# Expert blocks of a routed feed-forward layer as two 64-row halves, each with an expert of its own

## The reference

```
logits = einsum('th,eh->te', x, gate_w)            # 1024 tokens, 16 experts
scores = softmax(logits); topk_w, topk_idx = top_k(scores, 2)
combine = sum(one_hot(topk_idx, E) * topk_w[..., None], axis=1)
gu = einsum('th,ehj->etj', x, w_gate_up)           # 256 -> 2 x 176
h  = silu(gu[..., :I]) * gu[..., I:]
y  = einsum('eti,eih,te->th', h, w_down, combine)  # 176 -> 256
y  = y + swiglu(x @ shared_gate_up) @ shared_down
```

## Time and profile before

| | us |
|---|---|
| median of 3 runs | 252.67 (252.64 to 252.76) |
| profiled execution | 252.71 |
| its span, first to last instruction | 250.7 |
| PE / PEld busy | 237.4 / 177.2 |
| DVE / ACT / POOL busy | 148.5 / 129.3 / 92.5 |

### The profile page before, as it was taken

How to read it: one execution, slowest core, us unless ns; L and a number is a source line. 1 busy time by engine, 2 the same in 40 slices (tenths; PEclk the granted TensorE clock), 3 DMA queues, 4 the chain that set the end, 5 groups by cost and what they waited for, 6 DMA issues and landing times.

```text
span 250.7 us, 5232 instructions
## 1 busy us (share of the span) xinstructions
PE 237.4 (95%) x1660; PEld 177.2 (71%) x1660; DVE 148.5 (59%) x452; ACT 129.3 (52%) x465; POOL 92.5 (37%) x110
## 2 busy tenths in 40 slices
PE   8969799999999999999999999799999999999995
PEld 6635475666766677898788787567777777777784
DVE  1568888887889856437896588653223232323184
ACT  2146988989889898540524216124343434343440
POOL 2111211112111100102662004655777777777460
PEclk9999999999999999999999999999999999999999
DMA  7999877100005400006013000222333333343495
GB/s 217 267 366 387 283 174 171 53 3 3 3 0 160 171 3 3 1 3 229 1 41 129 0 3 4 63 68 81 105 105 107 105 95 112 89 102 111 144 338 188
DMA packets 20388, 28.10 MB, mean 112 GB/s; under 512 B 2369, under 2 KB 17355, under 8 KB 20363
## 3 DMA queue, kind: packets, MB, share of 16 engines
q1 hardware_dynamic: 16683, 19.01, 24.5%
q0 software_dynamic: 2976, 8.13, 11.0%
q10 hardware_dynamic: 704, 0.64, 0.8%
HBM read 21.61 MB, written 6.16 MB: 111 GB/s over the span
## 4 chain that ended last, share of the span: by engine, by line
PE 71%; ACT 13%; DVE 8%; issue 4%; DMA 1%; POOL 1%; ACTq 0%; POOLq 0%; DVEq 0%
PE bank L898 15%; PE bank L910 11%; ACT pr_s L1010 10%; PE bank L829 8%; PE bank L531 5%; PE bank L573 4%; PE bank L560 3%; PE bank L879 3%; PE bank L889 3%; PE bank L658 2%; PE bank L536 2%; PE bank L623 2%; PE bank L649 1%; PE bank L668 1%; DMA qx_s<-ffn_in,prT 1%
## 5 line engine op out<-in xcount | busy, mean ns | idle before, releaser
L1010 ACT ACTIVATE pr_s<-bank,mx 128x128 f32<-128x128 f32 x128 | 45.2, 383 | 8.0 <-DVE mx L1236 8.0
L898 PE MATMUL bank<-gu_s,bxT 128*128 x124 | 41.7, 460 | 0.2 <-DVE bxT L1561 0.2
L1567 DVE TENSOR_TENSOR pr_s<-bank,pr_s 128x176 f32<-128x176 f32 x31 | 10.6, 341 | 51.6 <-ACT pr_s L1165 50.9
L492 POOL DMA_INDIRECT expert_out<-by,prT x31 | 31.0, 1000 | 14.8 <-ACT by L1000 7.5
L487 POOL DMA_INDIRECT qx_s<-ffn_in,prT x31 | 30.1, 972 | 14.6 <-issue 8.2
L1000 ACT ACTIVATE prT<-bank 128x512 f32<-128x512 f32 (+1 forms) x63 | 31.1, 497 | 2.9 <-PE bank L573 1.8
L910 PE MATMUL bank<-dn_s,prT 88*128 x124 | 31.7, 379 | 0.0
L1010 ACT ACTIVATION_READ_ACCUMULATOR pr_s<-bank,mx 128x1 f32 x128 | 28.6, 224 | 0.0
L898 PEld LDWEIGHTS bank<-gu_s,bxT 128*128 128x128 f32 x124 | 21.2, 190 | 7.2 <-issue 0.4
L1000 ACT ACTIVATE by<-bank 128x256 f32<-128x256 f32 x31 | 11.9, 383 | 23.5 <-PE bank L910 21.9
L1236 DVE TENSOR_REDUCE mx<-bank 128x4 f32<-128x512 f32 x32 | 20.5, 683 | 4.7 <-PE bank L560 4.7
(11 more groups left out here) (194 smaller groups left out, 438.2 us busy)
## 6 DMA issues: line engine op xcount, KB each, us to landing
gu_s<-in_w_gu SPq DMA_DIRECT2D x8, 704.0 KB, 7.0
dn_s<-in_w_dn SPq DMA_DIRECT2D x4, 704.0 KB
gu_s<-in_ctx_in SPq DMA_DIRECT2D x2, 512.0 KB, 9.2
ffn_in<-x_s SPq DMA_DIRECT2D x4, 256.0 KB, 2.4
cv_s<-expert_out SPq DMA_DIRECT2D x4, 256.0 KB, 4.1
x_s<-expert_out SPq DMA_DIRECT2D x4, 256.0 KB, 5.7
out<-x_s SPq DMA_DIRECT2D x7, 128.0 KB, 3.6
gu_s<-in_x_t SPq DMA_DIRECT2D x1, 768.0 KB, 10.7
```

What stands on the lines that cost most here:

```text
L492: pool.indirect_dma_start(expert_out[:], bass.IndirectOffsetOnAxis(ap=idx[:, 1, k:k + 1], axis=0), by[:, k % RB, :], None).then_inc(dma_sc ...
L898: last = mm(bank[2 + i % 2][:, 0:2 * I], bxT[:, i % 2, k, :], gu_s[:, k, bass.ds(e, 1), :], start=k == 0, stop=k == KD - 1)
L1010: last = nc.scalar.activation(pr_s[:, n % 2, h, :], score_bank(n)[:, h * T:(h + 1) * T], ACT.Exp, bias=mx[:, n % 4, h:h + 1], accum_out=de ...
```

## The change

Blocks keep 128 rows but are made of two halves of 64, each with an expert of its own. The slots of an expert are now counted in halves of 64. The first half of expert e is the upper half of block e, for e = 0 to 15, at a fixed place, so the upper half's weights of these blocks need no register. All further halves (at most 32) are dealt out: one each to the lower halves of blocks 0 to 15, two each to blocks 16 to 23 (`more_of`). So 24 blocks always do. The lower half takes its weights by the register as before. The upper half of blocks 16 to 23 takes them from `gu_x`, `dn_x`, a ring of four (`SB`) that SP fills from memory, in a place where buffers of the attention stages lay (`first_half`). The two halves are separate products to output rows 0 to 63 and 64 to 127 of the same bank. The weights lie in memory in an order in which both k parts of a row follow each other. Further: three register reads move from before `shared_up(3, 0)` into it, and it moves ahead of `block_transpose(0)`; the slot table's products are halved too; one of GpSimd's two scalings goes to DVE; the routing arithmetic has a few more and wider operations.

```diff
-BLOCKS = (SLOTS + E * (T - 1)) // T
+HT = T // 2
+MORE = 2 * ((SLOTS - 1) // HT // 2 + 1)
+BLOCKS = E + (MORE - E) // 2
+HALVES = 2 * BLOCKS
+THRESHOLDS = B * T // HT - 1
+SB = 4
+def more_of(i):
+    return i if i < E else E + 2 * (i - E)
...
+        staged = early[0][:, 0:SB * (KD * 2 * I + 2 * D)].rearrange("p (r n) -> p r n", r=SB)
+        gu_x = staged[:, :, 0:KD * 2 * I].rearrange("p r (k n) -> p r k n", k=KD)
+        dn_x = staged[0:IH, :, KD * 2 * I:].rearrange("p r (k n) -> p r k n", k=2)
...
@@ sync, after the writes of ffn_in @@
+            sp.wait_ge(dve_block_experts, 1)
+            for j in range(BLOCKS - E):
+                d = more_of(E + j) + 1
+                e = sp.value_load(bei[0:1, d:d + 1], min_val=0, max_val=E - 1)
+                if j >= SB:
+                    sp.wait_ge(pe_expert_down, E + j - SB + 1)
+                sp.dma_start(gu_x[:, j % SB], w_gu[bass.ds(e, 1), :, :, :].rearrange("e p k n -> p (e k) n")).then_inc(dma_staged[j % SB], 16)
+                sp.dma_start(dn_x[:, j % SB], w_dn[bass.ds(e, 1), :, :, :].rearrange("e p k n -> p (e k) n")).then_inc(dma_staged[j % SB], 16)
             sp.wait_ge(dve_ring, 1)
@@ gpsimd @@
-            for k in range(2):
-                last = nc.gpsimd.tensor_tensor(num_b[:, 0, k * B:(k + 1) * B, :], num[:, k * B:(k + 1) * B, :],
-                                               tabr[:, R_TOK:R_TOK + B].unsqueeze(2).to_broadcast([128, B, BLOCKS]), ALU.mult)
-            last.then_inc(pool_block_numbers, 1)
+            nc.gpsimd.tensor_tensor(num_b[:, 0, 0:B, :], num[:, 0:B, :],
+                                    tabr[:, R_TOK:R_TOK + B].unsqueeze(2).to_broadcast([128, B, HALVES]), ALU.mult).then_inc(pool_block_numbers, 1)
@@ slot_table @@
-                            last = mm(bank[4][:, k * BLOCKS:(k + 1) * BLOCKS], hot[:, k * B + t, :],
-                                      num_b[:, f, k * B + t, :], start=t == 0 and f == 0, stop=t == B - 1 and f == 1)
+                            for u in range(2):
+                                last = mm(bank[4][u * HT:(u + 1) * HT, k * BLOCKS:(k + 1) * BLOCKS], hot[:, k * B + t, :],
+                                          num_b[:, f, k * B + t, u * BLOCKS:(u + 1) * BLOCKS],
+                                          start=t == 0 and f == 0, stop=t == B - 1 and f == 1, skip_group_check=True)
@@ expert_up @@
+                if i >= E:
+                    pe.wait_ge(dma_staged[(i - E) % SB], 32 * ((i - E) // SB + 1))
                 for k in range(KD):
-                    last = mm(bank[2 + i % 2][:, 0:2 * I], bxT[:, i % 2, k, :], gu_s[:, k, bass.ds(e, 1), :],
-                              start=k == 0, stop=k == KD - 1)
+                    mm(bank[2 + i % 2][0:HT, 0:2 * I], bxT[:, i % 2, k, 0:HT], gu_s[:, k, bass.ds(e, 1), :],
+                       start=k == 0, stop=k == KD - 1, skip_group_check=True)
+                    last = mm(bank[2 + i % 2][HT:T, 0:2 * I], bxT[:, i % 2, k, HT:T],
+                              gu_s[:, k, i, :] if i < E else gu_x[:, (i - E) % SB, k, :],
+                              start=k == 0, stop=k == KD - 1, skip_group_check=True)
@@ expert_down: the same in halves, with dn_s and dn_x @@
@@ tensor, before the loop @@
+            pe.wait_ge(dve_block_experts, 1)
+            shared_up(PAIRS - 1, 0, between=range(RB - 1))
             block_transpose(0)
-            pe.wait_ge(dve_block_experts, 1)
-            for i in range(RB - 1):
-                read_expert(i)
             pe.wait_ge(ld_gate_up, 16 * 8)
             pe.wait_ge(ld_down, 16 * 4)
-            shared_up(PAIRS - 1, 0)
             block_transpose(1)
@@ vector, routing @@
-            link(V.tensor_scalar_mul(nb[:, 2, :], nb[:, 1, :], float(T)))
+            link(V.scalar_tensor_tensor(nb[:, 2, :], nb[:, 1, :], float(HT), tabr[:, R_BASE:R_BASE + E], ALU.mult, ALU.add))
...
-            link(V.tensor_tensor(t128[:, 0], bank[2][:, 0:B * E].rearrange("p (t e) -> p t e", e=E),
-                                 nb[:, 2, :].unsqueeze(1).to_broadcast([128, B, E]), ALU.add))
+            link(V.scalar_tensor_tensor(t128[:, 0], rank, float(HT), nb[:, 2, :].unsqueeze(1).to_broadcast([128, B, E]),
+                                        ALU.is_ge, ALU.mult))
+            link(V.tensor_tensor(t128[:, 1], rank, t128[:, 0], ALU.add))
...
+            link(V.scalar_tensor_tensor(posf[:, 0, :], s8[:, 2:4, :].rearrange("p k t -> p (k t)"), float(HT), posf[:, 0, :],
+                                        ALU.mult, ALU.add))
...
+            V.tensor_tensor(num_b[:, 0, B:2 * B, :], num[:, B:2 * B, :],
+                            tabr[:, R_TOK:R_TOK + B].unsqueeze(2).to_broadcast([128, B, HALVES]), ALU.mult).then_inc(dve_slot_hot, 1)
```

More of the change, by code:

```diff
@@ L13 @@
+import math
 import numpy as np
@@ L85, in routing_constants @@
     p = np.arange(128)[:, None]
-    c[:, R_THR:R_THR + B] = 128.0 * np.arange(B)
+    c[:, R_THR:R_THR + THRESHOLDS] = HT * (1.0 + np.arange(THRESHOLDS))
     c[:, R_LOW:R_LOW + E * E] = (np.arange(E)[None, :] < np.arange(E)[:, None]).reshape(1, -1)
-    c[:, R_BLK:R_BLK + BLOCKS] = np.arange(BLOCKS)
-    c[:, R_SLOT:R_SLOT + T] = np.arange(T)
+    lower = [E + more_of(i) for i in range(BLOCKS)]
+    upper = [i if i < E else E + more_of(i) + 1 for i in range(BLOCKS)]
+    c[:, R_BLK:R_BLK + HALVES] = lower + upper
+    c[:, R_SLOT:R_SLOT + HT] = np.arange(HT)
+    c[:, R_MORE:R_MORE + MORE] = np.arange(MORE)
+    c[:, R_BASE:R_BASE + E] = E * HT - HT - HT * np.arange(E)
     c[:, R_TOK:R_TOK + B] = T * np.arange(B)
     c[:, R_TOK + B:R_TOK + 2 * B] = p + 1
-    c[:, R_RING:R_RING + RB] = RB - 1 - np.arange(RB)
+    c[:, R_RING:R_RING + RB] = E + 1 + 2 * (RB - 1 - np.arange(RB))
+    c[:, R_RING + RB:R_RING + 2 * RB] = 2 * E + 2 * (RB - 1 - np.arange(RB))
     c[:, R_DUMMY:R_DUMMY + BLOCKS] = DUMMY + T * np.arange(BLOCKS) + p + 1
@@ L131, in decoder_layer, with first_half @@
         halfpow = sb("halfpow", [128, B])
-        wq_s = sb("wq_s", [128, QW])
-        wkv_s = sb("wkv_s", [KPH, 2, NOPE + D])
-        wout_s = sb("wout_s", [128, KD, D])
+        early = [sb("early", [128, QW + 2 * (NOPE + D) + 3 * KD * D + XH * HD + 4 * KD * D + 2 * (QP + KP) + 2 * T + 4 * T])[:], 0]
+        def first_half(*shape):
+            flat, at = early
+            early[1] = at + math.prod(shape)
+            part = flat[:, at:early[1]]
+            if len(shape) == 2:
+                return part.rearrange("p (a b) -> p a b", a=shape[0])
+            if len(shape) == 3:
+                return part.rearrange("p (a b c) -> p a b c", a=shape[0], b=shape[1])
+            return part
+        wq_s = first_half(QW)
+        wkv_s = first_half(2, NOPE + D)[0:KPH]
+        wout_s = first_half(KD, D)
         lnq_s = tab[:, C_LN:C_LN + 2]
         lnkv_s = tab[0:KPH, C_LN + 2:C_LN + 6].rearrange("p (k n) -> p k n", k=2)
-        wh_s = sb("wh_s", [128, XH, HD])
-        wg_s = sb("wg_s", [128, KD, D])
-        wo_s = sb("wo_s", [128, KD, D])
+        wh_s = first_half(XH, HD)
+        wg_s = first_half(KD, D)
+        wo_s = first_half(KD, D)
         gn_s = sb("gn_s", [128, KD, 2])
@@ L255, in decoder_layer @@
         dve_ring = sem("dve_ring")
+        dma_staged = [sem(f"dma_staged{i}") for i in range(SB)]
         dve_first_sum, dve_second_sum, dma_out = sem("dve_first_sum"), sem("dve_second_sum"), sem("dma_out")
@@ L817, in logits_transpose, with shared_up @@
                 last.then_inc(pe_logits, 1)
-            def shared_up(q, c, halves=(0, 1)):
+            def shared_up(q, c, halves=(0, 1), between=()):
                 n, r = SC * q + c, shared_rows(c)
@@ L831, in shared_up @@
                                   xfT[:, k, 2 * q:2 * q + 2, :].rearrange("p b t -> p (b t)"), start=k == 0, stop=k == KD - 1)
+                        for i in between[KD * j + k:KD * j + k + 1]:
+                            read_expert(i)
                 if 1 in halves:
@@ L860, in slot_table @@
             def slot_table():
-                pe.wait_ge(dve_slot_hot, 1)
+                pe.wait_ge(dve_slot_hot, 2)
                 pe.wait_ge(pool_block_numbers, 1)
@@ L909, in expert_down @@
                 for k in range(2):
-                    last = mm(bank[4 + i % 2][:, 0:D], bhT[:, i % 2, k, :], dn_s[:, k, bass.ds(e, 1), :],
-                              start=k == 0, stop=k == 1)
+                    mm(bank[4 + i % 2][0:HT, 0:D], bhT[:, i % 2, k, 0:HT], dn_s[:, k, bass.ds(e, 1), :],
+                       start=k == 0, stop=k == 1, skip_group_check=True)
+                    last = mm(bank[4 + i % 2][HT:T, 0:D], bhT[:, i % 2, k, HT:T],
+                              dn_s[:, k, i, :] if i < E else dn_x[:, (i - E) % SB, k, :],
+                              start=k == 0, stop=k == 1, skip_group_check=True)
                 last.then_inc(pe_expert_down, 1)
@@ L1644 @@
         "gate": _np.pad(g["L0_ffn_gate_w"].T, ((0, 0), (0, 32 - E))),
-        "w_gu": g["L0_ffn_w_gate_up"],
-        "w_dn": g["L0_ffn_w_down"],
```

(2 more changed lines are left out.)

66 lines of the change are left out of this document (34 added, 32 removed).

## The result

| | before | changed |
|---|---|---|
| median, us | 252.71 (252.64 to 253.08) | 280.35 (279.39 to 281.61) |
| ratio | 1 | 1.109 (1.104 to 1.114) |
| profiled execution / its span | 252.71 / 250.7 | 279.39 / 277.6 |
| mean granted clock | 1.00 | 0.93 |

Slower by 11%, where 5.8% was forecast. The sign, the round of the loop and the four stalls are as predicted. The lower clock that comes with the stalls was a rival in the prediction and not a term of its sum, and the time lies 1.4 us above the upper end of the range. A ratio is estimated from the single runs, with its 95% interval, so it can differ by up to 0.004 from the quotient of the medians. All figures are of runs in the fast state; one run of f9_all_end, at 253.53 us, was slow and is left out of them.

A forecast was written before the change was run, and what follows sets the result against it. PE was taken to bound the kernel at 2.49 us per block; sixteen rounds of 3.09, four stalled rounds near 6.3 and an 18.6 end gave a 265.6 span, 267.3 us (range 254 to 279).

The forecast's parts named there:

- the four stalls: Blocks 20 to 23: PE waits for refills tied to expert_down four blocks earlier, 3.3 us each, 13.2 in all.
- Seven blocks less: Expert loop: 31 blocks become 24, 17.4 us off if a block still costs 2.49.
- halves side by side: Up and down products: the two 64-column halves overlap fully, no cost for the streaming.
- a product in turn: Rival, up and down: halves run one after the other, 2.06 more per block, about 316 us; chance 0.06.
- Edges: Loop: changes between whole and divided array, two round trips of 0.30 per block, 0.60 in all, 14.4 for 24 blocks.
- The end: After down(20): scatter, read-back, weighing and last shared product set the end, not PE; 18.6 us.
- the list of signs: Closing list of trace signs; for the end, PE idle between last downs and last shared products while DVE weighs.
- Clock: Rival, blocks 20 to 23 and end: pauses drop PE to 1.2 GHz, 275 us at two thirds; chance 0.14.
- the cases without stalls: Rivals at blocks 20 to 23: no stall, 254.1 us, chance 0.08; faster, stalls mostly missing, 249, chance 0.06.
- Landing and waking: Refills for blocks 20 to 23: 3.6 us for landing and waking both queues (2.5 to 4.3), 0.1 to up's start.
- Opening: Before the first up: routing, slot table, GpSimd, register reads and staging against gathers, net +0.3 us (-1.3 to +2.5).
- one pass in turn: Rival, up and down: one pass per stage stays alone, 12 us in all, 279 us; chance 0.05.

The follow-up runs named there:

- f9_all_end: Changed kernel plus separate up/down semaphores, staging held back, block transposes ahead of up, DVE's shared products ahead of weighing: 249.93 us, ratio 0.951.
- e4: Kernel before, 31 blocks, only up and down products cut into halves, upper half with another expert's weights: 269.44 us, ratio 1.064.
- g4: Kernel before with halved products, both transposes ahead of up and down, so two array changes per round, not four: 261.58 us, ratio 1.033.
- e1: Changed kernel with separate semaphores for staged up and down weights, each refilled after its own last reader: 254.93 us, ratio 1.006.
- e2: Changed kernel with 17 dummy products on PE ahead of the staged-weight wait of blocks 20 to 23: 273.02 us, ratio 1.075.
- e3: Changed kernel with staging of the first four slots held back until block 7 is transposed: 276.89 us, ratio 1.091.
- e7: Kernel before with register reads moved into shared_up(3, 0), and that ahead of block_transpose(0): 261.90 us beside 263.44, ratio 0.994.
- the second and third group: Two sets of follow-up runs in which the unchanged kernel before stood at 263 us; read by their ratios.

## Why the prediction was off in size

**Right.** *Seven blocks less and halves side by side*: rounds of 3.07, no sign of a product in turn. *Edges*: 0.58 for 0.60 in a round; the rows of attention lines with groups of 32 columns carried over to groups of 64. The Trainium skill ("TensorEngine Tiling (Array Packing)", Key Properties) says that only changing the mode drains the engine; e4 and g4 agree, and put 0.13 to 0.15 us on each change. (That every edge of the trace before paid the same 0.09 was misread: the prediction's own working has 0.09 to 0.20. The sum used 0.30 for a way in and out and was not touched by it.) *The place of the stalls*: four, behind down(16) to down(19), none before.

**The end: right in its number, partly by luck.** It took 18.4 from down(20) for 18.6, with the first read-back issued 3.1 after it, and scatter, read-back and weighing are on the chain as forecast. But PE was not idle in between, as the list of signs had it: at the lower clock its downs and shared products lasted until the weighing, and it waited 0.2 us. In e1, where PE is in time, it waits 5.3 us and then does its last 8 pieces at the lower clock in 4.00 us, and the end takes 20.2. In the changed kernel the clock was back at 0.97 for the last products (272 to 277.6).

**Clock: the step that failed.** The text had the size (two thirds of 12: 8; measured 7.3 by e2, 8.3 by the stretches) but put it down as a rival with a chance of 0.14, because no row of before showed a pause. Yet the forecast itself made four pauses of 3.3 us, nearly three times the longest wait in the earlier trace rows; only the cases without stalls would be without them. The clock was then not an alternative to the forecast but a consequence of it, and a term of the sum: 275. The Trainium skill's page that the prediction named ("TensorE: Matmul & The Clock Gate", Part 1) says that an idle engine is put back to 1.2 GHz, and so stood on that side. The runs agree with it: 0.50 behind the second pause.

**Landing and waking, mis-sized.** 3.6 and 0.1 were put from a line through the earlier trace rows; 4.14 to 4.22 were measured, each time: 0.2 from the down's end to SP's first issue, 0.5 to the last, 3.3 to the landing, 0.2 to PE's start. From first issue to landing that is 3.8 where 3.5 were put, and for the waking of both queues 0.4 where 0.2 were. It is 0.5 four times, 1.9 in all. Upper end 4.3, so inside its bounds.

**Opening, mis-sized.** +0.3 net was put, with "0 to 2 us" for the staging that meets the gathers. The gathers' landing doubled, and e3 prices it at 3.3 to 3.5 us. The other terms were put too high: the slot table's 64 passes take 1.19 for 0.96, 0.2 more and not 0.9, and GpSimd's part 1.68, not 2.4; with e7's 1.2 for the register reads, e3's up(4) starts at 172.21, before the forecast's 173.7. So two errors partly cancelled. Measured at up(4), the opening is 1.8 over the forecast; rounds of 3.07 for 3.09 give 0.3 back by up(19).

**The range.** Its end of 279 was taken from a rival (one pass in turn), not from clock and upper bounds together: 267.3 + 8 for the clock + 2.8 for the landing + 2 for the opening = 280.1, within 0.3 us of what was measured. Terms that go with the forecast's own mechanism add up; they are not alternatives.

Open: what disturbed the second and third group, why before suffers from it more than the kernels with 24 blocks, and why the clock fell between 20 and 24 us in some executions.

## What to carry to other kernels

A wait that a change adds to PE is priced by its gap and by the clock behind it: if the sum itself has pauses that the trace of before never had, their consequences are terms, not rivals. Before a transfer is tied to the last reader of a buffer, look at which of its parts is free earlier: here a semaphore of its own for the up half, with its refill ahead, gave back some 23 us. And where products on part of the array stand between products on the whole of it, put those of one kind together, since the price is per change.

## What the runs showed of the hardware

- Changing between 128 columns and two groups of 64 costs 0.13 to 0.15 us each way, seen in the first product after the change; grouping halves it (rounds of 3.07 and 2.77).
- With a wait of PE of 3.9 us the granted clock fell from 1.00 to 0.5, and the products behind it took 0.57 for 0.29. Between the later pauses it came back near the end of a round, and not in every one. A wait of 2.4 us, in the opening, left it at 1.00. Filling the pauses with idle products kept it at 1.00 (7.3 us).
- Eight bulk transfers, 2.2 MB together, took the landing of small indirect gathers from 2.7 to 3.9 us up to 5.3 to 7.7, and later in the kernel one to 7.2.
- 541 KB in two transfers had landed 3.8 us after the first issue.
